# Conditioning merged into self attention's block: the order of the first loads and of x's normalisation in a transformer block

## The reference

```python
c_proj = jax.nn.silu(c) @ W_mod + b_mod                 # (16, 512) @ (512, 3072)
shift_a, scale_a, gate_a, shift_m, scale_m, gate_m = jnp.split(c_proj, 6, axis=-1)
x_norm = modulate(_ln(x), shift_a, scale_a)             # ln(x) * (1 + scale) + shift
qkv = x_norm @ W_qkv + b_qkv                            # then 16 heads of 32
x = x + gate_a[:, None] * (attention(q, k, v) @ W_proj + b_proj)
x = x + cross_attention(_ln(x) @ W_qc + b_qc, _ln(context) @ W_kvc + b_kvc) @ W_cproj + b_cproj
h = gelu(modulate(_ln(x), shift_m, scale_m) @ W_mlp1 + b_mlp1)
x = x + gate_m[:, None] * (h @ W_mlp2 + b_mlp2)
```

## Time and profile before

| | us |
|---|---|
| median of 3 runs | 2833.18 (2833.15 to 2834.59) |
| profiled execution | 2836.57 |
| its span | 2834.7 |
| TensorE busy | 2683.2 (95%) |
| DVE, ACT, POOL busy | 1735.6, 1119.0, 1302.6 |
| mean granted clock of TensorE | 0.971 |

### The profile page before, as it was taken

The page is one execution under the profiler, slowest core; times in us unless marked ns, Lnnn a source line. Parts: engine busy times, 40 slices in busy tenths (PEclk is TensorE's granted clock), DMA queues, the critical chain, the costliest instruction groups (busy, mean ns, idle before and its releaser), DMA issues. The chain is left out here.

```text
span 2834.7 us, 49951 instructions
## 1 busy us (share of the span) xinstructions
PE 2683.2 (95%) x18600; PEld 2148.8 (76%) x18600; DVE 1735.6 (61%) x3275; ACT 1119.0 (39%) x2183; POOL 1302.6 (46%) x1449
## 2 busy tenths in 40 slices
PE   3899999999978999999999999999869999999997
PEld 1778888888767778877878777787548888888886
DVE  3467777777735677777777777776744443444431
ACT  2244444444433445555555555554532112212110
POOL 0335445445431666676666766766830220220211
PEclk9799999999979999999999999999879999999999
DMA  5443544444533444334443444433530110111110
GB/s 177 99 106 108 128 126 124 125 117 117 147 96 95 110 114 109 106 106 114 112 109 105 109 111 108 108 98 86 142 109 27 45 49 27 45 52 34 42 41 23
DMA packets 168687, 269.79 MB, mean 95 GB/s; under 512 B 28800, under 2 KB 83072, under 8 KB 168432
## 3 DMA queue, kind: packets, MB, share of 16 engines
q1 hardware_dynamic: 165376, 259.26, 33.6%
q0 software_dynamic: 3072, 7.34, 0.8%
HBM read 111.04 MB, written 36.77 MB: 52 GB/s over the span
## 5 line engine op out<-in xcount | busy, mean ns | idle before, releaser
L1399 DVE TENSOR_REDUCE cross_nmax<-cross_sc_ps 112x1 f32<-112x750 f32 x512 | 459.3, 928 | 159.1 <-PE cross_sc_ps L1274 159.1
L1517 ACT ACTIVATE cross_prT<-cross_tr_ps 125x448 f32<-125x448 f32 x768 | 389.9, 544 | 152.8 <-PE cross_tr_ps L1293 145.0
L1564 POOL TENSOR_TENSOR cross_part<-cross_prT 125x448 f32<-125x448 f32 x252 | 290.9, 1154 | 148.7 <-PE cross_or_ps L1313 82.3
L932 POOL TENSOR_TENSOR self_psum<-self_prT 112x224 f32<-112x224 f32 x256 | 174.3, 681 | 364.2 <-ACT self_prT L840 199.2
L1293 PE MATMUL cross_tr_ps<-cross_qst,cross_kst 98*125 98x224 f32 x1536 | 312.6, 290 | 7.9 <-ACT cross_prT L1517 4.0
L1293 PEld LDWEIGHTS cross_tr_ps<-cross_qst,cross_kst 98*125 98x125 f32 x1536 | 243.1, 189 | 92.0 <-ACT cross_prT L1517 39.0
L1566 POOL TENSOR_TENSOR cross_part<-cross_part,cross_prT 125x448 f32<-125x448 f32 x252 | 292.8, 1162 | 19.8
L1959 ACT ACTIVATE mlp_hv<-mlp_h_ps,mlp_b 128x512 f32<-128x512 f32 x112 | 77.1, 689 | 522.0 <-PE mlp_h_ps L74 507.9
L1274 PE MATMUL cross_sc_ps<-cross_kst,cross_qst 96*112 96x500 f32 (+1 forms) x1024 | 271.9, 348 | 6.9 <-DVE cross_nmax L1399 3.8
L1876 DVE CAST mlp_hT_h<-mlp_hv 128x512 fp32r<-128x512 f32 x112 | 52.3, 467 | 323.1 <-ACT mlp_hv L1959 323.1
L840 ACT ACTIVATE self_prT<-self_st_ps 112x448 f32<-112x448 f32 x256 | 138.9, 544 | 217.0 <-PE self_st_ps L542 217.0
(11 more groups left out here) (220 smaller groups left out, 6645.3 us busy)
## 6 DMA issues: line engine op xcount, KB each, us to landing
cross_kst<-cross_nat_h SPq DMA_DIRECT2D x512, 93.8 KB, 2.2
cross_c_in<-in_context SPq DMA_DIRECT2D x96, 250.0 KB
cross_kst<-cross_nat_l SPq DMA_DIRECT2D x256, 93.8 KB, 2.2
cross_qst<-qc SPq DMA_DIRECT2D x192, 112.0 KB, 2.4
self_kst<-self_nat_h SPq DMA_DIRECT2D x128, 112.0 KB, 2.3
self_qst<-self_natq_h SPq DMA_DIRECT2D x128, 112.0 KB, 3.0
self_x_in<-in_x SPq DMA_DIRECT2D x16, 448.0 KB, 3.7
self_kst<-self_nat_l SPq DMA_DIRECT2D x64, 112.0 KB, 2.3
```

Source lines behind the costliest of these rows:

```text
L932: pool.tensor_tensor(psum[:, j], prT[:, j, 0], prT[:, j, 1], ALU.add).then_inc(p_summed, 1)
L1399: dve.tensor_reduce(nmax[:, g % 2, t, j:j + 1], sc_ps[t][0:QN, SC0:SC0 + S], AX_X, ALU.max, negate=True).then_inc(maxed, 1)
L1517: act.activation(prT[:, slot(h), 2 * c:2 * c + 2], bank((h + LAG) % NH, c)[0:SN, 0:2 * N].rearrange("p (k t) -> p k t", k=2), ACT.Exp).the ...
L1564: pool.tensor_tensor(part[:], prT[:, j, 0:2], prT[:, j, 2:4], ALU.add).then_inc(pre_summed, 1)
```

## The change

The two blocks ahead are gone, and their work stands in self attention's own block. SP loads cond, x of batch 0 and b_mod, then W_mod's shift and scale of attention in halves, then W_qkv in the order k, q, v, each piece into the place of its low part (raw views in `wqkv_raw`, `wproj_raw`, `wqc_raw`), x of batch 1 once x of batch 0 has been turned, the other four pieces of W_mod, and b_proj; W_proj and W_qc follow the stacking of batch 0. W_mod and b_mod lie in tiles that later hold something else (kst, qst, x_res and others). Shift and scale of attention are made as rows and turned; those of the MLP are made directly as columns with W_mod as the stationary operand (`modulation`, five products of 16 columns for each 128 channels), between q and v, together with the transposes of batch 1; the gates follow the first score. The splits of k, q and v are spread over the first loop, those of W_proj and W_qc over the first eight steps of batch 0. `weights_ready` makes TensorE wait for each piece at its first use.

```diff
-def constants_phase(nc, ident, neg_half, eps):
-def condition_phase(nc, cond_t, w_mod, b_mod, gates, mod_t, ident, parts, columns):
-def split_views(parts, stage):
-def load_phase(nc, phase, parts, columns):
...
-        condition_phase(nc, cond_t, w_mod, b_mod, gates, mod_t, ident,
...
+        wqc_raw = nc.alloc_sbuf_tensor_at("self_wqc_raw", [P, KC, H], F32, offset=wqc_at + 4 * KC * H)
+        wm_late = nc.alloc_sbuf_tensor_at("self_wm_late", [P, 4, KC, H], F32, offset=late_at)
+        wm = nc.alloc_sbuf_tensor_at("self_wm", [P, 2, KC, H], F32, offset=kst_at)
+        bm = nc.alloc_sbuf_tensor_at("self_bm", [B, 6 * H], F32, offset=qst_at + 4 * HPG * KC * N)
...
+        MOD = (SHIFT_A, SCALE_A, SHIFT_M, SCALE_M, GATE_A, GATE_M)
+        mod_raw = [wm[:, 0], wm[:, 1]] + [wm_late[:, i] for i in range(4)]
+        MOD_BANK = (sc_ps[0], sc_ps[1], st_ps[1], st_ps[1], st_ps[0], or_ps)
+        FIRST_TX = (tx_ps, or_ps)
+
+        CHUNKS = [(wqkv_raw[:, k, at:at + H], wqkv[0][:, k, at:at + H], wqkv[1][:, k, at:at + H], f)
+                  for at, f in ((H, 1.0), (0, SCALE), (2 * H, 1.0)) for k in range(KC)]
+        CHUNKS += [(wproj_raw[:, k], wproj[0][:, k], wproj[1][:, k], 1.0) for k in range(KC)]
+        CHUNKS += [(wqc_raw[:, k], wqc[0][:, k], wqc[1][:, k], SCALE) for k in range(KC)]
+        WEIGHTS = {"k": 0, "q": KC, "v": 2 * KC, "p": 3 * KC, "c": 4 * KC}
...
+                if b.c == 0:
+                    sp.wait_ge(gates_out, 32)
...
+            def load_mod(i):
+                m = MOD[i]
+                sp.dma_start(mod_raw[i], w_mod[:, m * H:(m + 1) * H].rearrange("(k p) n -> p k n", p=P)).then_inc(wm_in[i - 2], 16)
+
+            def load_first_mod(i):
+                src = w_mod[:, MOD[i] * H:(MOD[i] + 1) * H].rearrange("(k p) n -> p k n", p=P)
+                for half in range(2):
+                    at = slice(2 * half, 2 * half + 2)
+                    sp.dma_start(mod_raw[i][:, at], src[:, at]).then_inc(first_in[i][half], 16)
+
+            def load_w(kind, src, at):
+                for k in range(KC):
+                    i = WEIGHTS[kind] + k
+                    sp.dma_start(CHUNKS[i][0], src[k * P:(k + 1) * P, at:at + H]).then_inc(w_in[i], 16)
+
+            sp.dma_start(cond[:], cond_t).then_inc(cond_in, 16)
+            sp.dma_start(x_in[:], x[0].rearrange("(t p) n -> p t n", p=QN)).then_inc(x_first, 16)
+            sp.dma_start(bm[:], b_mod.rearrange("(a n) -> a n", a=1).broadcast_to([B, 6 * H])).then_inc(bm_in, 16)
+            load_first_mod(0)
+            load_first_mod(1)
+            load_w("k", w_qkv, H)
+            sp.dma_start(bqkv[:], b_qkv_t).then_inc(columns_in, 16)
+            sp.dma_start(bqc[:], b_qc_t).then_inc(columns_in, 16)
+            load_w("q", w_qkv, 0)
+            load_w("v", w_qkv, 2 * H)
             load_x(Batch(1))
+            for i in range(2, 6):
+                load_mod(i)
+            sp.dma_start(bproj[:], b_proj.rearrange("(a n) -> a n", a=1).broadcast_to([QN, H])).then_inc(bproj_in, 16)
             stack(Batch(0), k_l, nat, kst, k_stacked, (0, 1, 0))
             stack(Batch(0), q_l, natq, qst, q_stacked, (0, 0, 1))
+            load_w("p", w_proj, 0)
+            load_w("c", w_qc, 0)
+            for n in range(2):
+                sp.wait_ge(rows_done, n + 1)
+                sp.dma_start(gates[n], vt[0:B, 1, n]).then_inc(gates_out, 16)
...
+            def weights_ready(kind, c, part, o, k):
+
+                if o.c == 0 and c == 0 and (part == 0 or kind in "vp"):
+                    pe.wait_ge(w_l, WEIGHTS[kind] + k + 1)
...
+                    pe.wait_ge(mod_done, 2)
+                    pe.wait_ge(rows_done, 2)
...
-            for c in range(2):
-                wait(pe, xT_v, c)
-                trans(x_in, c, xhat1, Batch(0), xT_ps)
+            def modulation(i):
+                pe.wait_ge(wm_in[i - 2], 16)
+                for m in range(KC):
+                    at = (i % 2 * KC + m) * B
+                    for k in range(KC):
+                        pe.matmul(MOD_BANK[i][:, at:at + B], mod_raw[i][:, k, m * P:(m + 1) * P], silu[:, k], start=k == 0, stop=False)
+                    last = pe.matmul(MOD_BANK[i][:, at:at + B], bm[0:1, MOD[i] * H + m * P:MOD[i] * H + (m + 1) * P], ones[0:1, 0:B],
+                                     start=False, stop=True)
+                last.then_inc(mod_ps, 1)
+            def modulation_rows(i):
+                for k in range(KC):
+                    if i < 2 and k % 2 == 0:
+                        pe.wait_ge(first_in[i][k // 2], 16)
+                    elif k == 0:
+                        pe.wait_ge(wm_in[i - 2], 16)
+                    last = pe.matmul(MOD_BANK[i][0:B, :], silu[:, k], mod_raw[i][:, k], start=k == 0, stop=k == KC - 1)
+                last.then_inc(mod_ps, 1)
+            pe.wait_ge(silu_done, 1)
+            modulation_rows(0)
+            pe.wait_ge(shaped, 1)
+            trans(x_in, 0, xhat1, Batch(0), xT_ps, FIRST_TX[0])
+            modulation_rows(1)
+            trans(x_in, 1, xhat1, Batch(0), xT_ps, FIRST_TX[1])
+            for n in range(2):
+                pe.wait_ge(mod_rows, n + 1)
+                for k in range(KC):
+                    at = (n * KC + k) * B
+                    last = pe.transpose(st_ps[0][:, at:at + B], vt[0:B, 0, n, k * P:(k + 1) * P], ident[0:B, 0:B])
+            last.then_inc(mod_turned, 1)
             start = Batch(-1)
             for h in range(NH):
                 for f in fills(start, h, "kqvpc"):
                     fill(start, *f)
-                for _, c, _, o in fills(start, h, ("tx",)):
-                    turn_x(start, c, o)
+                if h == 6:
+                    pe.wait_ge(constant, 1)
+                    modulation(2)
+                    turn_x(start, 0, Batch(1))
+                    modulation(3)
+                    turn_x(start, 1, Batch(1))
             score(Batch(0), 0)
+            modulation_rows(4)
+            modulation_rows(5)
...
+                bank = FIRST_TX[c] if b.c == 0 else tx_ps
...
+                    if b.c == 0 and h < 2 * KC:
+                        low_w(3 * KC + h)
...
+            def low_w(i):
+                raw, high, low, factor = CHUNKS[i]
+                dve.wait_ge(w_h, i + 1)
+                dve.scalar_tensor_tensor(out=low, in0=raw, scalar=factor, in1=high.bitcast(F32), op0=ALU.mult,
+                                         op1=ALU.subtract).then_inc(w_l, 1)
+            def first_rows(i, one):
+                dve.wait_ge(mod_ps, i + 1)
+                dve.scalar_tensor_tensor(out=vt[0:B, 0, i], in0=MOD_BANK[i][0:B, :], scalar=one, in1=bm[:, MOD[i] * H:(MOD[i] + 1) * H],
+                                         op0=ALU.add, op1=ALU.add).then_inc(mod_rows, 1)
+            def gate_rows(i):
+                dve.wait_ge(mod_ps, i + 1)
+                dve.tensor_tensor(vt[0:B, 1, i - 4], MOD_BANK[i][0:B, :], bm[:, MOD[i] * H:(MOD[i] + 1) * H], ALU.add).then_inc(rows_done, 1)
+            def keep_first_modulation():
+                dve.wait_ge(mod_turned, 1)
+                dve.tensor_copy(mod_t[:, 0:2 * KC], st_ps[0][:, 0:2 * KC * B].rearrange("p (m b) -> p m b", b=B)).then_inc(mod_done, 1)
+                dve.wait_ge(mod_done, 1)
+            def keep_modulation():
+                columns = MOD_BANK[2][:, 0:2 * KC * B].rearrange("p (m b) -> p m b", b=B)
+                dve.wait_ge(mod_ps, 4)
+                dve.tensor_copy(mod_t[:, 2 * KC:3 * KC], columns[:, 0:KC])
+                dve.tensor_scalar(mod_t[:, 3 * KC:4 * KC], columns[:, KC:2 * KC], 1.0, None, ALU.add).then_inc(mod_done, 1)
+            a = Batch(0)
+            dve.wait_ge(exp_done, 1)
+            dve.tensor_scalar(cond_d[:], cond_e[:], 1.0, None, ALU.add).then_inc(den_done, 1)
+            dve.wait_ge(den_done, 1)
+            dve.reciprocal(cond_i[:], cond_d[:]).then_inc(inv_done, 1)
+            dve.wait_ge(inv_done, 1)
+            dve.tensor_tensor(silu[:], cond[:], cond_i[:], ALU.mult).then_inc(silu_done, 1)
+            stats(a, x_in, x_first, lambda t: 16, st1, mv1, stats1, mvs1)
+            neg_mean(a, mv1, rs1, nm1, rstd1, nmr1)
+            dve.wait_ge(bm_in, 16)
+            first_rows(0, 0.0)
+            low_w(0)
+            low_w(1)
+            first_rows(1, 1.0)
+            keep_first_modulation()
+            for c in range(2):
+                modulate(a, c)
+            for i in range(2, KC):
+                low_w(i)
+            dve.wait_ge(columns_in, 32)
             dve.tensor_scalar(bqs[:], bqkv[:, 0:KC], SCALE, None, ALU.mult)
             dve.tensor_scalar(bqcs[:], bqc[:], SCALE, None, ALU.mult).then_inc(bias_scaled, 1)
             dve.wait_ge(bias_scaled, 1)
-            a = Batch(0)
-            stats(a, x_in, x_loaded, lambda t: 0, st1, mv1, stats1, mvs1)
-            neg_mean(a, mv1, rs1, nm1, rstd1, nmr1)
-            for c in range(2):
-                modulate(a, c)
             start = Batch(-1)
             for h in range(NH):
```

(70 more changed lines are left out.)

170 lines of the change are left out of this document (34 added, 136 removed).

## The result

| | before | changed |
|---|---|---|
| median, us | 2833.16 (2832.38 to 2834.59, 4 runs) | 2805.49 (2803.65 to 2808.78, 4 runs) |
| profiled execution, us | 2836.57 | 2803.65 |
| its span | 2834.7 | 2801.5 |
| mean granted clock | 0.971 | 0.973 |

The ratio is 0.9903, with a 95% interval of 0.9886 to 0.992: 27.7 us faster, where 42.8 were forecast. The time lies 2.5 us above the range's upper end of 2803. On the two profiled executions the difference is 32.9.

The account below looks back on a forecast made before the run. TensorE bounds the kernel, so time can be won at the head only: -48.7 (K) + 0.5 (MLP modulation) + 6.9 (gates) - 3.0 (clock) + 1.5 (DVE) = -42.8, a median of 2790.4 us; range 2782 to 2803.

Parts of the forecast that it names:

- K: Start of self attention's first product in the head: forecast at 22.3 us, 48.7 earlier than before.
- The sign for wrong load steps: If the first product with W_mod starts behind 10 us, the load steps are wrong; about 7 was expected.
- The rival of late loads: W_mod mixed with the weights behind it: K at 25 to 29, time 2793 to 2797; chance 0.20.
- SP's queue: Between K and S: SP free at 24.9, wanted at 33.3; stacking issues beginning behind 36 would show the queue wrong.
- S: Start of the first score: forecast at 50.9, as K's 22.3 plus 28.1 as before plus 0.5.
- The MLP's modulation: 80 short instructions ahead of v on TensorE: 6.0 us against 6.3 of slack, 0.5 put on the path.
- The bound of 20: Upper price of the MLP's modulation, from x's transposes at the lower clock, 0.25 each; would put 14 on the path.
- Only a rival: Lower clock stays through v and gates: MLP modulation +5, gates 13.7, the 3.0 not saved; 2805, chance 0.11.
- the good case's 3.4: All goes well: k's products at the high level save 3.4 and DVE does not bind; 2785, chance 0.14.
- lies beside this: Between K and S: v's copy, batch 1's transposes and POOL's 6 us memset said to lie beside TensorE's work.
- The gates: 16 modulation instructions between the first score and the rest of batch 0: 6.9 us, nothing hides them.
- Behind S: Batch 0: 3.0 us saved by TensorE's clock, 1.5 lost to weight splits on DVE in its first eight steps.

Follow-up runs that it names:

- both edits: Changed kernel with the MLP's shift and scale made as rows and POOL's memset of kst moved behind its work for batch 1's x: 2791.78 us, ratio 0.9853.
- one gate moved: Kernel with both edits, the MLP gate's product moved from behind the first score to behind step 12 of batch 0: 2788.41 us, ratio 0.9847.
- The doubled piece: Changed kernel with the second piece of the MLP's modulation issued twice in a row, as columns: 2819.24 us (one run).
- the piece behind v: Changed kernel with the second piece of the MLP's modulation moved behind v, ahead of the first score: 2800.78 us (one run).

## Why the prediction was wrong

- **K.** Forecast 22.3, measured 23.25. The first half of W_mod let TensorE start at 8.83 and not at 7.0, since it landed 6.7 after issue, not 4.9 (the four halves took 6.6 to 9.1). The shift products took 6.0 (6.2 forecast), x was ready ahead of their end, scale's rows took 3.6. The sign for wrong load steps, a start behind 10, did not come. The rival of late loads would have had K at 25 to 29, and is out. Right within 0.9, which is less than the 1.1 by which K differs between executions.
- **SP's queue.** Forecast free in time, the stack's first issue wanted at 33.3. SP had issued all that stands ahead at 25.0 (24.9 forecast). The first issue went at 35.50, within the 36 given (34.21 and 32.74 where the scalings aren't held), and the last was twelve microseconds ahead of S. Right.
- **The MLP's modulation: the step that failed.** The text took 6.0 us for the 80 instructions and put 0.5 of it on the path, against 6.3 of slack. They took 14.7 (5.4 and 9.3), so 8.4 went beyond the slack. The row that was chosen, the transposes of 16 columns at 0.075 each, was chosen by what it streams. An instruction of the new form takes 0.131 at the high level and 0.235 at the lower. What bounds it looks like the loading: PEld is as busy as PE (1.78 and 1.89 in the rows at 50.42), and a load takes 0.186 to 0.337, one of the transposes 0.138. That is argued, not shown, since no run changes the load alone. The row that fits is a product of k, which also loads 128 by 128: in the changed kernel they start 0.11 apart at 23.46 and 0.21 apart at 25.15, and both were there in the kernel before (0.21 at 71.39, 0.11 at 78.20). 80 of these would be 8.8 to 17, with 14.7 between them. The bound of 20 stood in the text, but the range went by 5 for this rival. The Trainium skill ("TensorE: Matmul & The Clock Gate", LDWEIGHTS) gives 107 ns for a weight load of 128 columns, an estimate of 8.5 us for all 80. The trace has 131 an instruction at the high level, so the page was nearer than the chosen row, and still 6 us short of what the clock made of it. The sign given, that this term is wrong if the modulation takes over 8 us, came.
- **The clock between K and S.** Only a rival had it, with 0.11. It said that the clock stays low through v and the gates. The first part came, and larger. The second did not: v's products, 0.63 each up to 58.06 and 0.40 from there, brought the clock back, at the cost of 1.0, and the gates ran at 1.00. So its 2805 met the measured median by one of its three terms, with losses elsewhere in place of the other two; that is luck and no confirmation. Of the good case's 3.4 for k's products at the high level nothing came: from 24.0 to 30.8 they ran at 0.50 again.
- **The memset "lies beside this".** It was costed at nothing as work of another engine. It held DVE's scalings for 5.6 us, ACT's eviction of k waited 6.02 for them, and TensorE 1.62 at 34.21. In the kernel before, the scalings stood ahead of x's statistics, eleven microseconds from the memset:

```profile
62.40 0.17 DVE L783 TENSOR_SCALAR self_bqs<-self_bqkv 128x4 f32<-128x4 f32 x1 [2.21 <-PEq L93]
...
73.33 6.07 POOL L985 MEMSET self_kst<- 2x7168 f32 x1
```

  The path from K to the first piece was 16.4, and 14.5 before: 1.9. With 8.4 for the MLP and 1.0 for v that makes 11.3; measured are 11.1 over the 28.1 of the earlier trace rows.
- **The gates.** Forecast 6.9, measured 7.0, with TensorE coming warm out of v. Right.
- **Behind S.** Forecast -3.0 for the clock and +1.5 for the splits. From the first fill of batch 0 (29.9 earlier than before) to SP's load of the residual (159.21 before, 124.52 now, 34.7 earlier) the lead grew by 4.8 in the profiled pair. In the changed kernel run again it was 2.5. The clock behind S is at 1.00, as forecast. For the splits the trace has one wait of 0.2, so 1.5 looks too much; no run leaves them out. This is the one part that went better than the sum, and the 2.3 between the two executions are the stretch at 0.54 from 102.5 to 110.5.
- **Profile and median.** The sum was made against a profiled execution 3.4 above its median, and the same distance was taken for the changed one. That one's profiled execution lay 1.8 below its median. Of the 15.1 us of the miss 5.2 are this step, and 9.9 the terms above: 0.9 for K, 10.6 between K and S, 3.3 back in batch 0, and 1.5 that the lead loses again later; that makes 9.7.

What stays open: why the clock fell 3.4 us into the 16-column form with the memset moved, and 4.6 to 5.2 into it in the four runs without; why a load of these products takes longer than one of the transposes, since the bias products, which load one partition by 128, take as long as the others (0.260 in the mean); where 1.5 us of the lead go between 125 us and the end, which is within what executions of one kernel differ by there; and why the shift products took 1.1 less in some executions (both edits, one gate moved), so that K differed with the same code.

The kernel with both edits shows the rest of the working sound. With its products in the form that the earlier trace rows had priced, the gain came within 1.0 of the forecast, and K to S took 28.5 to 29.1, where 28.6 were forecast. That S itself came within 0.2 is in part luck: where K was 23.3, it was 52.4, 1.5 behind the forecast.

## What to carry to other kernels

Price a matmul of few columns also from a row that loads the same shape, not only from one that streams the same. When the two differ as here (6.0 against 8.8 to 17), let the range hold both. And ask what clock level it leaves to its neighbours; if the short side can be the one that is held (16 rows by 512 columns), it took 3.5 us for each piece here where the other form took 5.4 to 9.3. An operation costed at nothing because it is on another engine needs a look at what else touches the same memory at that moment, above all when the change moves either of the two. A sum made on one profiled execution should give the distance to the median a width of its own, some 3 us here on each side.

## What the runs showed of the hardware

- TensorE busy without a break can fall to 1.2 GHz: granted 0.50 from 45 to 55 us, with 5.00 of 5 us busy, on products of 16 columns with weights of 128. The doubled piece kept it there for 9.4 us more, with a DMA share of 0.01 beside it. It was back at 1.00 during products of 512 columns (from 58.1 in the changed kernel; in the kernel with the piece behind v from 48 on, and the next piece then ran at 0.131 an instruction).
- A memset of 6.07 us on POOL (two partitions, 7168 elements each) held DVE's one-input scalings of four columns until its end: started at 25.22 and 25.29, over at 30.90 and 30.91, where alone they take 0.16. Splits with two inputs weren't held (0.63 each). But beside POOL's subtraction of x's low part, which reads two tiles, two splits took 3.14 (the row at 22.15) where the two at 15.56 had taken 1.27, and the two subtractions took 2.67 together, where each had taken 1.13 in the kernel before. The Trainium skill has this rule ("SBUF — State Buffer", Who interferes with whom): VectorE and GpSimd share one pair of ports; a one-input operation in the mode that uses both pairs of ports is locked out by a GpSimd instruction that came first until that ends, and one with two inputs meets only GpSimd instructions that read. The three cases here agree (in which mode the scalings ran, no view shows), and this rule, had it been weighed, would have pointed at the memset.
- Executions of the same code differ in pace. At the end of batch 0 the granted clock was back at 1.00 from 102.5 to 110.5 us in one execution of the changed kernel and at 0.54 in the other, 2.3 us of time. In W_mod's first eight products the step from 0.85 to 0.43 us an instruction came at 13.8 in one kernel and at 11.9 in another with the same code there, 1.1 us of time, and the view gives 1.00 for all of it.
